# State-space stage: first pieces made ahead of the second chunk, side products and ScalarE's copies in another order

## The reference, cut to what matters

```python
normed = rmsnorm(x, input_norm_w)
x_z, z = split(normed @ in_proj_W)              # E = 256 each
xc = silu(conv1d(x_z) + conv_b)                 # 4 taps, per channel
dt = clip(softplus(xc @ dt_W + dt_b), 0.001, 0.1)
Bp, Cp = xc @ B_W, xc @ C_W                     # N = 64 each
def step(h, ins):                               # over the 64 tokens
    h = exp(dt_t[..., None] * A) * h + dt_t[..., None] * B_t[:, None, :] * x_t[..., None]
    return h, einsum('ben,bn->be', h, C_t)
y = scan(step)(...) * silu(z)
x = x + y @ out_proj_W
```

## Time and profile before

| | |
|---|---|
| median of 3 runs | 6143.91 us (6141.46 to 6144.05) |
| the profiled execution, its own time | 6141.57 us |
| span of the profiled execution | 6139.9 us |
| mean granted TensorE clock | 0.927 |
| busy: TensorE, VectorE, ScalarE, GpSimd | 5048.8, 4765.8, 3362.9, 3323.3 us |
| `mamba` | from the start to about 2300 us |

### The profile page before, as it was taken

How to read it: one execution, slowest core, us unless ns; L and a number is a source line. 1 busy time by engine, 2 the same in 40 slices (tenths; PEclk the granted TensorE clock), 3 DMA queues, 4 the chain that set the end, 5 groups by cost and what they waited for, 6 DMA issues and landing times. The chain is left out here.

```text
span 6139.9 us, 170947 instructions
## 1 busy us (share of the span) xinstructions
PE 5048.8 (82%) x62308; PEld 2980.5 (49%) x62308; DVE 4765.8 (78%) x8035; ACT 3362.9 (55%) x5020; POOL 3323.3 (54%) x3129
## 2 busy tenths in 40 slices
PE   6999999999999986787876965999967758888890
PEld 2444444434444334565664633676655536666440
DVE  5999999999999995796866355777759949998334
ACT  4666666666666654455861211444447737887440
POOL 4444445544444314565752664555537748887674
PEclk8999999999999998898988986999988969999995
DMA  1111111111111113221122642000001111111443
GB/s 49 50 46 48 49 44 52 46 47 50 44 52 42 50 33 94 65 60 35 45 80 55 156 114 72 18 17 16 16 22 44 50 31 48 49 50 40 151 150 83
DMA packets 584082, 347.70 MB, mean 57 GB/s; under 512 B 63977, under 2 KB 562476, under 8 KB 583468
## 3 DMA queue, kind: packets, MB, share of 16 engines
q1 hardware_dynamic: 562268, 312.85, 18.0%
q0 software_dynamic: 11648, 21.26, 1.8%
q10 hardware_dynamic: 9552, 5.58, 0.3%
HBM read 180.39 MB, written 66.85 MB: 40 GB/s over the span
## 5 line engine op out<-in xcount | busy, mean ns | idle before, releaser
L1424 ACT ACTIVATE mb_dA<-ps,mb_a_neg 128x1024 f32<-128x1024 f32 x1008 | 1124.1, 1115 | 789.8 <-PE ps L1182 789.0
L1860 DVE TENSOR_TENSOR mb_m<-mb_dA,ps 128x704 f32<-128x704 f32 x1008 | 893.1, 886 | 32.0
L1867 DVE TENSOR_TENSOR ps<-mb_m,ps 128x704 f32<-128x704 f32 x992 | 881.2, 888 | 0.1
L1165 PE MATMUL ps<-mb_m,mb_ident 128*32 128x320 f32 x7936 | 741.3, 446 | 7.2
L1214 PE MATMUL ps<-mb_m,mb_cz 128*32 128x256 f32 x8064 | 622.7, 380 | 31.5 <-issue 14.6
L1854 DVE TENSOR_TENSOR mb_m<-mb_dA,ps 128x320 f32<-128x320 f32 x1008 | 484.7, 481 | 85.9 <-PE ps L1165 67.3
L1197 PE MATMUL ps<-mb_ur,mb_bl 64*128 64x256 bf16 x4032 | 388.1, 271 | 49.7 <-DVE mb_m L1860 42.8
L1214 PEld LDWEIGHTS ps<-mb_m,mb_cz 128*32 128x32 f32 x8064 | 255.5, 110 | 324.8 <-issue 56.0
L1182 PE MATMUL ps<-mb_ur,mb_sel 64*128 64x256 bf16 x4032 | 396.3, 275 | 18.0 <-DMA mb_ur<-mb_pc 12.6
L1720 POOL TENSOR_TENSOR mb_ys<-mb_ys,mb_cbu 128x256 f32<-128x256 f32 x64 | 46.9, 732 | 531.4 <-ACT mb_ys L1521 530.4
L712 POOL TENSOR_TENSOR ea_p<-ea_p,ea_rec 128x2048 f32<-128x2048 f32 x70 | 253.5, 3621 | 90.0 <-DVE ea_rec L858 90.0
(11 more groups left out here) (506 smaller groups left out, 13235.1 us busy)
## 6 DMA issues: line engine op xcount, KB each, us to landing
mb_ur<-mb_pc SPq DMA_DIRECT2D x768, 64.0 KB
mb_bl<-mb_pc SPq DMA_DIRECT2D x576, 64.0 KB
ef_w<-in_ef_w SPq DMA_DIRECT2D x35, 515.5 KB
mx_w<-in_mx_w SPq DMA_DIRECT2D x39, 384.0 KB
moe_made<-mx_y SPq DMA_DIRECT2D x39, 256.0 KB, 2.4
ea_x<-hidden SPq DMA_DIRECT2D x280, 32.0 KB, 2.0
pairs<-ea_y SPq DMA_DIRECT2D x70, 128.0 KB, 1.9
ef_tk<-pairs SPq DMA_DIRECT2D x35, 256.0 KB
```

Of the source, the lines that this page charges most:

```text
L1165: mm = nc.tensor.matmul(out[c:c + 32], weights[:, c:c + 32], moving, start=start, stop=stop, skip_group_check=not grouped)
L1424: nc.scalar.activation(dA[:, t % RING].rearrange("p (g n) -> p g n", g=2), ps[:, DT:DT + 2, :], ACT.Exp, scale=a_neg[:, 0:1]).then_inc(dA_ ...
L1860: nc.vector.tensor_tensor(m[:, t % RING, DVE_PART], dA[:, t % RING, DVE_PART], state(u, t - 1, DVE_PART), ALU.mult).then_inc(md_ready.sem, 1)
L1867: nc.vector.tensor_tensor(h, m[:, t % RING, DVE_PART], h, ALU.add).then_inc(hd_ready.sem, 1)
```

## The change

Four things. In `first`, the pieces of the first two quarters are made between chunk 0's and chunk 1's projections, on TensorE and ScalarE, and SyncE issues the transfers of a piece when that piece is there. In the steps, `turn_u` and `project_bc` of the second quarter come one step later, `gates` one step earlier, and `project_c` has one piece in each of the steps 13, 14 and 15. On ScalarE `take_y`, `take_c`, `take_u`, `take_bc`, `take_turned`, `take_turn`, `take_gates`, `take_conv` and `take_dt` stand ahead of the step's `decay`. And `weigh_bc` is done by ScalarE, as an activation with an accumulated output, not by VectorE as a reduce.

```diff
+    UT = [1, 2, 1, 1]
...
+                def spread_first(j):
+                    for q, ready in enumerate((hi_ready, mid_ready, lo_ready)):
+                        sp.wait_ge(ready.sem, ready.at(j))
+                        sp.sem_inc(sp_passed.sem, 1)
+                        for a in range(3):
+                            sp.dma_start(ur[3 * q + a:128:16, j], pc[:, j, q, 0:E]).then_inc(pieces_loaded.of(j), 16)
+                            sp.dma_start(bl[3 * a + q:128:16, j], pc[:, j, q, 2 * E:3 * E]).then_inc(pieces_loaded.of(j), 16)
+                        sp.dma_start(ur[9 + q:128:16, j], pc[:, j, q, E:2 * E]).then_inc(pieces_loaded.of(j), 16)
...
-                    spread_pieces(0, 0)
-                    spread_pieces(0, 1)
+                    for j in range(2):
+                        spread_first(j)
...
                     for i in range(2):
                         if i == 1:
-                            pe.wait_ge(cn_ready.sem, cn_ready.at(0))
+                            for j in range(2):
+                                pe.wait_ge(cn_ready.sem, cn_ready.at(0))
+                                if j == 1:
+                                    pe.wait_ge(bc_taken.sem, bc_taken.at(0))
+                                turn_u(0, j)
+                                project_bc(0, 0, j)
+                            pe.wait_ge(bc_taken.sem, bc_taken.at(1))
                         turn(i)
...
-                    turn_u(0, 0)
-                    project_bc(0, 0, 0)
-                    pe.wait_ge(bc_taken.sem, bc_taken.at(0))
-                    turn_u(0, 1)
-                    project_bc(0, 0, 1)
                     products((0, 1), (0, 0), 0)
                     products((0, 2), (0, 1), 0)
-                    pe.wait_ge(bc_taken.sem, bc_taken.at(1))
...
+                    if tl == UT[j] and ahead:
...
+                    if tl == UT[j] + 1 and ahead:
...
-                            elif tl == 10:
+                            elif tl == 9:
                                 pe.wait_ge(xT_ready.sem, xT_ready.at(i + 2))
-                            if tl in (10, 11, 12, 13):
-                                gates(i + 2, tl - 10)
-                        if lead and tl == 14:
-                            if lead >= 2:
+                            if tl in (9, 10, 11, 12):
+                                gates(i + 2, tl - 9)
+                        if lead and tl >= 13:
+                            if lead >= 2 and tl == 13:
                                 pe.wait_ge(gates_taken.sem, gates_taken.at(i + 2))
-                            project_c(i + 1, 1 - u, 0)
-                            project_c(i + 1, 1 - u, 1)
-                        if lead and tl == 15:
-                            project_c(i + 1, 1 - u, 2)
+                            project_c(i + 1, 1 - u, tl - 13)
...
+                def weigh_bc(i, j):
+                    k = 4 * i + j
+                    act.wait_ge(cb_step.sem, cb_step.at(k))
+                    act.wait_ge(cbu_ready.sem, cbu_ready.at(k - 1))
+                    nc.scalar.activation(cb_prod[:], cb_prod[:], ACT.Identity, accum_out=cb[:, 0:1]).then_inc(cb_ready.sem, 1)
...
                     for i in range(2):
+                        if i == 1:
+                            act.wait_ge(zeroed.sem, zeroed.at(0))
+                            lay_c(0, 0, 0)
+                            for j in range(2):
+                                take_u(0, j)
+                                take_bc(0, j)
+                                round_hi(0, j)
+                                round_mid(0, j)
+                                weigh_bc(0, j)
                         take_turn(i)
...
                 def chunk(i, u, lead, trail):
                     for t in range(T):
                         j, tl = t // 16, t % 16
-                        if t + 3 < T:
-                            decay(i, t + 3)
-                        elif lead and t + 3 > T:
-                            decay(i + 1, t + 3 - T)
+                        ip, jp = (i, j + 2) if j < 2 else (i + 1, j - 2)
                         behind = j > 0 or trail
-                        if j == 1 and tl == 0 and lead:
-                            take_c(i + 1, 1 - u)
                         if tl == 0 and behind:
                             if j == 0:
                                 take_y(i - 1, 3)
                             else:
                                 take_y(i, j - 1)
+                        if j == 1 and tl == 0 and lead:
+                            take_c(i + 1, 1 - u)
                         if j < 2 or lead:
-                            ip, jp = (i, j + 2) if j < 2 else (i + 1, j - 2)
-                            if tl == 1:
+                            if tl == UT[j]:
                                 take_u(ip, jp)
-                            elif tl == 2:
+                            elif tl == UT[j] + 1:
                                 take_bc(ip, jp)
-                            elif tl == 5:
-                                round_hi(ip, jp)
-                            elif tl == 7:
-                                round_mid(ip, jp)
                         if tl == 4 and behind:
                             if j == 0:
                                 take_turned(i - 1, 3)
                             else:
                                 take_turned(i, j - 1)
+                        if j == 0 and lead >= 2:
+                            if tl == 8:
+                                take_turn(i + 2)
+                            elif tl in (10, 12):
+                                take_gates(i + 2, (tl - 10) // 2)
+                        if j in (1, 2) and lead >= 2 and tl == 15:
+                            take_conv(i + 2, j - 1)
+                        if j == 3 and lead >= 2 and tl in (11, 15):
+                            take_dt(i + 2, (tl - 11) // 4)
+                        if t + 3 < T:
+                            decay(i, t + 3)
+                        elif lead and t + 3 > T:
+                            decay(i + 1, t + 3 - T)
+                        if j < 2 or lead:
+                            if tl == 5:
+                                round_hi(ip, jp)
+                            elif tl == 7:
+                                round_mid(ip, jp)
+                            elif tl == 11:
+                                weigh_bc(ip, jp)
                         if tl == 9:
...
-                        if j == 0 and lead >= 2:
-                            if tl == 8:
-                                take_turn(i + 2)
-                            elif tl in (11, 13):
-                                take_gates(i + 2, (tl - 11) // 2)
-                        if j in (1, 2) and lead >= 2 and tl == 15:
-                            take_conv(i + 2, j - 1)
                         if j in (2, 3) and lead >= 2 and tl == 3:
                             tanh_of_x(i + 2, u, j - 2)
-                        if j == 3 and lead >= 2 and tl in (11, 15):
-                            take_dt(i + 2, (tl - 11) // 4)
                         if j == 3 and lead >= 3 and tl in (6, 8, 10, 12):
...
-                def weigh_bc(i, j):
-                    k = 4 * i + j
-                    dve.wait_ge(cb_step.sem, cb_step.at(k))
-                    dve.wait_ge(cbu_ready.sem, cbu_ready.at(k - 1))
-                    nc.vector.tensor_reduce(cb[:], cb_prod[:], AX.X, ALU.add).then_inc(cb_ready.sem, 1)
...
-                        if tl == 11:
-                            if j < 2:
-                                weigh_bc(i, j + 2)
-                            elif lead:
-                                weigh_bc(i + 1, j - 2)
```

More of the change, by code:

```diff
@@ L1332, in side @@
                     behind = j > 0 or trail
-                    if tl == 1 and ahead:
+                    if tl == UT[j] and ahead:
                         if j == 0 and lead:
@@ L1345, in side @@
                             turn_u(i + 1, j - 2)
-                    if tl == 2 and ahead:
+                    if tl == UT[j] + 1 and ahead:
                         if j < 2:
@@ L1553, in first @@
                                 tanh_of_z(0, 0, half)
-                    act.wait_ge(zeroed.sem, zeroed.at(0))
-                    lay_c(0, 0, 0)
-                    for j in range(2):
-                        take_u(0, j)
-                        take_bc(0, j)
-                        round_hi(0, j)
-                        round_mid(0, j)
                     decay(0, 1)
@@ L1889, in first @@
                     split_lo(0)
-                    weigh_bc(0, 0)
                     own_rows(1)
@@ L1893, in first @@
                     split_lo(1)
-                    weigh_bc(0, 1)
                     gate_x(1)
```

## The result

The changed kernel takes **6087.96 us**, the median of 4 runs (6086.91 to 6095.11); the kernel before took 6143.98 us on the same chip (4 runs, 6141.46 to 6145.72). The ratio is 0.991, with a 95% interval from 0.9894 to 0.9925. The forecast was 6086. The profiled execution took 6088.12 us, span 6086.5, mean granted clock 0.927.

A forecast was written before the change was run, and what follows sets the result against it. VectorE was taken to set the pace, 2.125 us a step, with 4.1 us of extras a chunk. Loop 48.9 plus prologue 7.1 gave 56.0 us off 6141.57, forecast 6086 us, range 6078 to 6110.

The forecast's parts named there:

- reduce: Steps with weigh_bc: taking the reduce off VectorE saves 0.125 us in 62 steps, 7.8 us.
- start of 2nd quarter: Second quarter of 15 chunks: the 1.87 us wait behind take_y goes, saving 28.0 us.
- `take_u` (t = 3, 35, 51): Quarters 0, 2, 3 of 15 chunks: project_bc's wait for take_u goes, 0.21 us each, 9.5 us.
- t = 15: Step 15 of a chunk: VectorE's 0.43 us wait, after project_c pieces behind take_gates, goes 14 times, 6.0 us.
- `take_dt`: Chunk's end: standing ahead of decay(2), it costs 0.2 us about 12 times, -2.4 us.
- turning of the loop: Hardware loop's turning back: no term in the sum; another cost there would show the forecast wrong.
- first step: Prologue: the first dt product, which VectorE's first step awaits, comes 3.5 us sooner.
- `project_dt`: Two groups between steps 1 and 2: 1.83 us each instead of 3.64 at the higher clock, saving 3.6 us.
- the waits move but stay: Rival for the loop: TensorE's load is the reason, only reduce and prologue win, 15 us, 6129 us; chance 0.10.
- margin of 0.41 us: Plain step: TensorE idle 0.41 us ahead of decay's product, so other copies ahead of decay cost nothing.
- First product: Prologue's first dt product: at 72.9 us instead of 76.44, with conv's clock loss taken as 2.3 us.
- The first rival, the clock staying low: Prologue: TensorE at 1.2 GHz all through, product at 79.6, gain 45.7 us, total 6096 us; chance 0.15.

The follow-up runs named there:

- e1: Kernel before with only weigh_bc's reduce moved from VectorE to ScalarE: 6189.35 us, against 6167.50 before on the same chip.
- e8: Changed kernel with the reduce back on VectorE: 6126.76 us, against 6177.41 for the kernel before on the same chip.
- e2: Kernel before with only ScalarE's copies put ahead of the step's decay: 6132.36 us, against 6167.50 before on the same chip.
- e9: Changed kernel with TensorE's side work and its copies back in their old steps, copies still ahead of decay: 6119.68 us, against 6177.41 before.
- e3: Kernel before with only TensorE's side work and its copies in the new steps, copies still behind decay: 6181.13 us, against 6167.50 before.
- e7: Changed kernel with take_dt behind decay again: 6117.10 us, against 6174.91 for the kernel before on the same chip.
- e4: Kernel before with only the new prologue and transfers issued per piece: 6163.01 us, against 6167.50 before on the same chip.
- e10: Changed kernel with an added 256-column ScalarE copy ahead of every decay: 6133.13 us, against 6177.41 for the kernel before on the same chip.
- e6: Changed kernel with 18 unread matmuls in the prologue's gaps to hold TensorE's clock up: 6115.81 us, against 6174.91 before on the same chip.
- e11: Changed kernel with 13 unread prologue matmuls, chunk 2's norms and scaling moved, six chunks per hardware-loop body: 6109.76 us, ratio to before 0.9888.
- e5: Changed kernel with each set's prologue transfers issued only after the third piece: 6107.37 us, against 6174.91 before on the same chip.
- c_after: The changed kernel itself, rerun on another chip: 6113.50 us, against 6174.91 for the kernel before there, ratio 0.9902.

## Why the forecast was right, step by step

The total came within 2 us of the forecast, and that close it is by luck: the stage gained 3.9 us more than the sum, and the later stages took 6 us more. Inside the stage, too, some terms were wrong and cancelled. The chunk is the fairest test: 134.41 measured, 134.5 forecast.

| term | forecast | measured in the loop | what the runs say |
|---|---|---|---|
| reduce | 7.8 | 7.4 | only with the new order: e1 +1.7, e8 9.7 |
| start of 2nd quarter | 28.0 | 27.9 | order alone (e2); places not needed (e9) |
| `take_u` (t = 3, 35, 51) | 9.5 | 10.9 | order alone |
| t = 15 | 6.0 | 7.7 | order alone; places alone too, but they make new waits (e3) |
| `take_dt` | -2.4 | about -0.4 | against the other place a gain of 0.11 a chunk (e7) |
| turning of the loop | 0 | 0.8 | 11.1 to 10.3 us, the four chunks at the two turns over plain ones; the other runs with two turns have 9.6 to 11.5, so this is spread |
| t = 10 of chunk 0 | 0 | -1.7 | unseen; comes with the order (e2) |
| first step | 3.5 | 2.0 | start-up, GpSimd, clock |
| `project_dt` | 3.6 | 4.0 | e4 too |

Each number of the loop is the excess of that step over 2.125 us, summed over 16 chunks, before minus after. They add to 58.6 of the 59.9; the rest lies in many small ones.

**The loop.** The central claim holds: the extras of a chunk were waits for ScalarE's copies, not TensorE's load. TensorE is still busy 130.60 of 134.41 us, and the rival "the waits move but stay" is refuted for the full change. It is what happened to two of its parts, though. Taken alone on the old order, the reduce and TensorE's places each moved their waits and won nothing (e1, e3). The forecast costed the terms one by one and added them. That was harmless only because the one part on which the others rest, the order, was in the change. And it named TensorE's places as part of the cause for 34 us, in the steps on the start of a quarter and on `gates` and `project_c`; e2 and e9 show that the order alone does it.

`take_dt` was the term with the wrong argument: 2.4 us of cost forecast, 0.4 measured at t = 1, and against the place behind `decay` a gain. The argument was that 0.68 us would stand before a `decay` that is on the path. e7 shows why not: ahead of `decay` the copy runs while ScalarE would have waited for the `dt` product, and behind it the copy delays the next `decay`. The wait at t = 2 is 1.11 us, 1.09 before; 1.3 was forecast.

The margin of 0.41 us, on which the other copies were costed at nothing, was read off a row of PEld, TensorE's load of weights; its matmuls ran up to that product without a gap. What the trace of the kernel before shows is this:

```profile
2192.03 1.11 ACT L1424 ACTIVATE mb_dA<-ps,mb_a_neg 128x1024 f32<-128x1024 f32 x1 [0.49 <-PE ps L1182]
...
2193.72 0.39 PE L1182 MATMUL ps<-mb_ur,mb_sel 64*128 64x256 bf16 x4
```

`decay` ends at 2193.14 and the next product starts at 2193.72, so by these rows `decay` may be up to about 0.6 us late, an estimate. The conclusion held, for another number; e10 tested 0.3 us of it.

**The prologue.** First product 74.6 against 72.9. The chain was laid out rightly, and each of three links was longer: `du` was complete 0.7 us later, which is start-up that this change doesn't touch; `turn_u` to the second `round_mid` took 13.9 us for 13.1; and the clock cost 2.7 us in conv for 2.3. The 0.8 us of the second link add up from longer and shorter parts: the first `project_bc` took 1.08 us instead of 0.64 at the lower clock, VectorE was some 0.8 us slower while GpSimd's gates ran beside it (below), and `cbu` took 1.34 us instead of 0.92, while 0.9 were saved because the first `weigh_bc` no longer stands behind `split_lo`, which the forecast had taken as even. The first rival, the clock staying low, did not occur: it was at 1.00 from 67 us on, and `project_dt` gained its 3.6 us and a little more. e6 adds what the forecast did not have: the clock can be held up there, for 1.7 us at the first step, but it can fall again at the wait for GpSimd at t = 10, and then 1.5 of them are gone. In e11, without that wait, the clock stays at 1.00 from 96 to 104 us.

**The rest of the span.** 6 us of the stage's gain are not in the total. Behind the last `mb_y`, windows of both kernels (the first row is of before, the second of after):

```profile
2311.00:6139.90 3828.90, 2914.58 (x31652) 2066.40 (x31652) 2621.35 (x4859) 1907.55 (x3159) 2316.64 (x2135) 0.89 0.22 63
```

```profile
2251.40:6086.50 3835.10, 2915.63 (x31652) 2070.18 (x31652) 2622.35 (x4859) 1907.45 (x3159) 2318.62 (x2135) 0.89 0.22 63
```

The same instructions, busy for the same time to within 4 us on every engine. In all runs the gated MLP took between 132.7 and 135.3 us and the grouped attention between 757.9 and 777.7, in no order that follows the edits. Behind the last `mb_y` the twelve kernels took 3856.1 (e5) to 3875.0 us (e1); c_after took 3858.5, and the longest, e1, is all but the kernel before. And on c_after's chip the medians differ by 61.4 us, more than the stage gained, so no fixed loss of 6 us comes with the change. I take the 6 us as that spread; what makes the spread is open.

## What to carry to other kernels

In an engine's hand-written order, put a short copy that another engine waits for ahead of the long operation that itself still waits for its input: 46 of the 60 us came from that reordering alone. Cost such edits together: a part that wins 8 us with the order and nothing without it has no price of its own. After removing waits, look at the first rounds again: here the new order made the wait for GpSimd in chunk 0 1.7 us dearer, and e11 has it gone. And before a difference is put down to an edit, see where in the trace it arises: 1.6 of e7's 2.4 us lay ahead of anything that the edit moved.

## What the runs showed of the hardware

VectorE and GpSimd slow each other, and by much; in these rows one of them pays at a time. Timeline of the changed kernel; the same VectorE line stands once beside GpSimd's gates and once alone:

```profile
47.76 1.28 DVE L1845 TENSOR_TENSOR mb_cb_prod<-mb_bc_tok 128x64 f32<-128x64 f32 x1
...
55.09 0.22 DVE L1845 TENSOR_TENSOR mb_cb_prod<-mb_bc_tok 128x64 f32<-128x64 f32 x1
```

1.28 us against 0.22 for 64 columns (`own_rows`, L1841, 1.03 against 0.43), while GpSimd beside it took its usual 1.27 and 1.33 us. And GpSimd's L1671, 1.27 us elsewhere, took 4.13 us at 40.84 beside VectorE's `du` operations, which took what they took alone (1.29 us a pair). The Trainium skill (GPSIMD Engine Reference, "1. Specifications") says that GpSimd's interfaces to SBUF are shared with VectorE and that contention arises with VectorE's instructions of two SBUF inputs; the trace agrees, and gives the size. In the steps, where each of VectorE's operations has an operand in PSUM (0.48 and 0.89 us), GpSimd's work beside them costs nothing that the rows show.

A turn of the hardware loop costs about 5 us here (4.8 to 5.9 over plain chunks in the 14 profiles). At the first turn of the changed kernel TensorE is idle for 4.03 us and comes back at a lower clock; timeline and then a window:

```profile
760.94 0.85 PE L1224 MATMUL ps<-mb_m,mb_cz 128*32 128x256 f32 x8 [4.03 <-DVE mb_m L1872]
...
762.26 1.29 PE L1175 MATMUL ps<-mb_m,mb_ident 128*32 128x320 f32 x8
...
765.11 0.74 PE L1175 MATMUL ps<-mb_m,mb_ident 128*32 128x320 f32 x8
```

```profile
760.50:763.50 3.00, 2.56 (x21) 0.53 (x21) 0.39 (x1) 1.49 (x2) 2.73 (x3) 0.62 0.47 113
```

The granted clock is 0.62 over the 3 us, and the eight matmuls of `add_decayed` take 1.29 us, against 0.74 three microseconds later; at the second turn it is 0.61 (1305 to 1308 us). The Trainium skill (TensorE: Matmul & The Clock Gate, "What's actually happening") has an idle TensorE throttled to half; the trace agrees at both turns.

A short wait can be enough for the clock to fall, and need not be: behind the same 1.94 us of idle TensorE in chunk 0 it was 0.50 in e6 and 0.55 in e7, and 1.00 in c_after, and the runs with the fall lost 1.5 to 1.6 us by it.

And the same code differs between chips: 224 us for the mixture of experts on the first, 244 to 248 on the others, and the kernel before took 6143.98, 6167.50, 6174.91 and 6177.41 us on the four. A total from one chip can't be set beside one from another to judge 10 us.
